# Three narrow attention stages of an eight-layer kernel: score lanes regrouped into five slots, and extra matmuls at the head of a stage

## The reference, cut to what matters

```
q = norm(x) @ Wq + bq ; k = ctx @ Wk + bk ; v = ctx @ Wv + bv      # 16 heads of 8
p = softmax(q k^T * scale [+ mask])                                # 512 x 154 for a head
x = x + tanh(gate) * (p v @ Wo + bo)
```

## Time and profile before

| | us |
|---|---|
| median of the three runs | 2459.78 |
| the profiled execution | 2450.34 |
| its span, first to last instruction | 2448.6 |
| TensorE busy | 2070.1 (85%) |
| VectorE busy | 1224.5 (50%) |
| ScalarE busy | 702.1 (29%) |
| mean granted TensorE clock | 0.857 of full |

### The profile page before, as it was taken

The page is one execution under the profiler, slowest core; times in us unless marked ns, Lnnn a source line. Parts: engine busy times, 40 slices in busy tenths (PEclk is TensorE's granted clock), DMA queues, the critical chain, the costliest instruction groups (busy, mean ns, idle before and its releaser), DMA issues. The chain is left out here.

```text
span 2448.6 us, 33104 instructions
## 1 busy us (share of the span) xinstructions
PE 2070.1 (85%) x12226; PEld 1166.4 (48%) x12226; DVE 1224.5 (50%) x2940; ACT 702.1 (29%) x1245; POOL 93.2 (4%) x178
## 2 busy tenths in 40 slices
PE   4689799988898987987799788888888796997997
PEld 3343477763534435554544344444444554543554
DVE  5553222226655655554443364736364575342776
ACT  2332233332233331222132313142422222323221
POOL 0000000000000000000000101010101001000000
PEclk7777899999898998997597688898989876787999
DMA  1320000020000000000000000000000000000000
GB/s 35 111 77 6 1 0 0 0 48 17 0 0 0 0 0 0 0 0 6 14 9 1 0 1 2 1 2 1 1 1 1 1 0 14 14 1 1 1 0 17
DMA packets 36509, 23.68 MB, mean 10 GB/s; under 512 B 14275, under 2 KB 31896, under 8 KB 36405
## 3 DMA queue, kind: packets, MB, share of 16 engines
q1 hardware_dynamic: 34965, 21.93, 3.6%
q10 hardware_dynamic: 1440, 0.29, 0.1%
HBM read 16.04 MB, written 1.05 MB: 7 GB/s over the span
## 5 line engine op out<-in xcount | busy, mean ns | idle before, releaser
L1741 ACT ACTIVATE L2a_qwork<-psum 128x512 f32<-128x512 f32 (+3 forms) x256 | 94.5, 438 | 226.8 <-PE psum L1671 225.4
L452 DVE RECIPROCAL L1x_rsum<-psum 128x512 f32<-128x512 f32 x32 | 107.4, 3356 | 84.1 <-PE psum L343 84.1
L1842 DVE RECIPROCAL L2a_rsum<-psum 128x512 f32<-128x512 f32 x16 | 53.7, 3357 | 153.4 <-PE psum L1686 153.4
L1340 ACT ACTIVATE L0f_hid<-psum,L0f_b 128x512 f32<-128x512 f32 x128 | 87.9, 687 | 142.3 <-PE psum L1292 140.1
L395 ACT ACTIVATE L1x_pT<-psum 77x512 f32<-77x512 f32 x128 | 68.8, 587 | 193.8 <-PE psum L329 193.7
L1305 PEld LDWEIGHTS psum<-expert_arena,L0f_hid 128*128 128x128 f32 x1024 | 118.4, 192 | 12.0 <-issue 11.5
L1292 PE MATMUL psum<-L0f_xnT,expert_arena 128*128 128x512 f32 x256 | 122.7, 625 | 0.0
L1667 PE MATMUL psum<-L2a_qT,L2a_kT 64*128 64x128 f32 (+3 forms) x512 | 108.2, 506 | 15.2 <-ACT L2a_qwork L1741 10.7
L1305 PE MATMUL psum<-expert_arena,L0f_hid 128*128 128x128 f32 x1024 | 119.3, 275 | 0.0
L1455 DVE SCALAR_TENSOR_TENSOR L0f_acc<-psum,L0f_comb,L0f_acc 128x128 f32<-128x128 f32 x128 | 36.0, 344 | 159.4 <-PE psum L1305 159.4
L1824 DVE TENSOR_REDUCE L2a_negmax<-psum 128x2 f32<-128x256 f32 (+3 forms) x128 | 100.8, 821 | 24.3 <-PE psum L1639 24.3
(11 more groups left out here) (553 smaller groups left out, 3948.0 us busy)
## 6 DMA issues: line engine op xcount, KB each, us to landing
expert_arena<-in_L_ffn_w SPq DMA_DIRECT2D x16, 256.0 KB
L1f_gu<-in_L_ffn_gate_up_w SPq DMA_DIRECT2D x8, 256.0 KB, 4.1
resid<-in_x SPq DMA_DIRECT2D x4, 256.0 KB, 6.1
L0x_q<-L0x_qc SPq DMA_DIRECT2D x16, 64.0 KB
L1f_dn<-in_L_ffn_down_w SPq DMA_DIRECT2D x8, 128.0 KB, 4.2
expert_arena<-in_L_ffn_w_gate_up SPq DMA_DIRECT2D x2, 512.0 KB, 5.4
L2x_q<-L2x_qc SPq DMA_DIRECT2D x16, 64.0 KB
L3x_q<-L3x_qc SPq DMA_DIRECT2D x16, 64.0 KB
```

Source lines behind the costliest of these rows:

```text
L452: v.step(nc.vector.reciprocal(rsum[:, g % 2, :], psum[:, 2 * (g % 2) + 1, :]))
L1340: nc.scalar.activation(hid[0:rows, n % RING, :], psum[0:rows, n % 4, :], ACT.Relu, bias=bias).then_inc(s["hid"], 1)
L1741: nc.scalar.activation(pT[:, c % 2, j, PLACE[k]:PLACE[k] + WIDTH[k]], psum[:, 4 + n % 4, k * P:SEQ], ACT.Exp, scale=scale).then_inc(s["pt" ...
```

## The change

Within the three narrow stages:

- The transposed scores go in five slots for each batch. Slots 0 to 3 take the four row groups of one plane c side by side, into four banks (2 to 5). Slot 4 takes the last 26 keys as 16 tiles of 32 rows by 32 columns, straight from k4, so that `kbd` and GpSimd's work on it go. `values` is split into `products` and `sums`, which are called one slot later and apart from each other.
- Banks 2 and 3 are thereby taken from the score units. Every unit now writes banks 0 and 1, and unit n waits for the reduce of unit n - 1. The projections share bank 0 (`FRONT`) and bank 1 (`OUT`) with the units.
- The maxima go in halves of a batch (planes 0 and 1, then 2 and 3), with a `max_rows`, a copy and a DMA for each.
- `turned(f)` moves from the end of a batch to the head of the next one, behind `products` and `sums` of the last slot. VectorE's `squares` and `rotated` move with it, behind `normalised(b-1)`.
- `output(b-1)` comes after the first slot but one. bo and bv no longer cost one-row matmuls: GpSimd adds gate * (bv @ wo + bo) to the residual beforehand. wo is loaded with its rows regrouped.
- `warm(6)` at the head of the stage and `warm(4)` ahead of the first score units issue ten matmuls of 128x128 by 512 whose result is not used.

```diff
+    FRONT, SUMS, OUT = 0, 7, 1
...
+            def warm(n):
+
+                for _ in range(n):
+                    nc.tensor.matmul(psum[:, SUMS, :], core.ident[:], core.ctxT[:, 0:SEQ], start=True, stop=True)
+
+            warm(6)
...
-                    if n >= 2:
-                        pe.wait_ge(s["mx"], UNITS * f + n - 1)
+                    if n:
+                        pe.wait_ge(s["mx"], n)
...
-                            last = nc.tensor.matmul(psum[:, j, (t % 2) * CTX:(t % 2 + 1) * CTX], q4[rows, f % QB, c, t * P:(t + 1) * P],
+                            last = nc.tensor.matmul(psum[:, j % 2, (t % 2) * CTX:(t % 2 + 1) * CTX], q4[rows, f % QB, c, t * P:(t + 1) * P],
...
+                if c < NG:
+                    for j in range(NG):
+                        rows = slice(32 * j, 32 * j + 32)
+                        if n:
+                            pe.wait_ge(s["pt"], NG * (n - 1) + j + 1)
+                        nc.tensor.matmul(psum[:, 2 + j, :], k4[rows, b, c, 0:MAIN], q4[rows, b % QB, c, :], start=True, stop=True).then_inc(s["s2"], 1)
+                    return
+                for x in range(NG):
+                    for j in range(NG):
+                        rows = slice(32 * j, 32 * j + 32)
+                        if x == 0:
+                            pe.wait_ge(s["pt"], NG * (n - 1) + j + 1)
+                        last = nc.tensor.matmul(psum[32 * x:32 * x + 32, 2 + j, :], k4[rows, b, x, MAIN:KP], q4[rows, b % QB, x, :], start=True, stop=True)
```

More of the change, by code:

```diff
@@ L849, in _ @@
                 queries(0)
+                if masked:
+                    for x in range(2):
+                        last = nc.tensor.transpose(psum[0:64, 2, x * KH:(x + 1) * KH], pen_w[:, x].rearrange("p b h -> p (b h)"), core.ident[0:KH, 0:KH])
+                    last.then_inc(s["pen_ps"], 1)
+                if not rope:
+                    nc.tensor.matmul(psum[:, 6, 0:D], bvb[:], w["wo"][:], start=True, stop=True).then_inc(s["bias_ps"], 1)
                 turned(0)
+                contexts(1)
@@ new lines, in _ @@
+                    n = 16 * f
+                    scoresT(b, 0)
+                    if b:
+                        max_rows(2 * b + 1)
+                        products(b - 1, NG)
+                        sums(b - 1, NG)
+                    else:
+                        scores(8, 16)
+                    if f < B:
+                        turned(f)
+                    if b == 0:
+                        max_rows(1)
+                    scoresT(b, 1)
+                    if b:
+                        output(b - 1)
@@ new lines, in _ @@
+                    if f < B:
+                        scores(n, n + 2)
+                    products(b, 0)
+                    if f < B:
+                        scores(n + 2, n + 3)
+                    sums(b, 0)
+                    if f < B:
+                        scores(n + 3, n + 4)
+                    scoresT(b, 2)
+                    if f < B:
+                        scores(n + 4, n + 5)
+                    products(b, 1)
+                    if f < B:
+                        scores(n + 5, n + 6)
@@ new lines, in _ @@
+                    sums(b, 1)
+                    if f < B:
+                        scores(n + 6, n + 8)
+                    scoresT(b, 3)
+                    products(b, 2)
+                    if f < B:
+                        max_rows(2 * f)
+                    sums(b, 2)
+                    if f < B:
+                        scores(n + 8, n + 12)
+                    if g < B:
+                        contexts(g)
+                        rowsT(g)
+                    scoresT(b, 4)
+                    if g < B:
+                        queries(g)
@@ L880, in _ @@
+                    products(b, 3)
+                    if f < B:
+                        scores(n + 12, n + 13)
+                    sums(b, 3)
+                    if f < B:
+                        scores(n + 13, n + 16)
+                products(B - 1, NG)
+                sums(B - 1, NG)
                 output(B - 1)
```

485 lines of the change are left out of this document (232 added, 253 removed).

## The result

| | before | after |
|---|---|---|
| median of the runs | 2457.02 us (2449.64 to 2462.27) | 2537.5 us (2535.61 to 2541.84) |
| profiled execution, its span | 2450.3, 2448.6 | 2536.5, 2534.8 |
| granted clock, mean | 0.857 | 0.848 |
| L0x, L2x, L3x | 251.4, 234.0, 218.5 | 296.6, 245.6, 241.9 |

The ratio is 1.0332, with a 95% interval of 1.03 to 1.0365: slower. The three narrow stages are 45.2 + 11.6 + 23.4 = 80.2 us longer, of the span's 86.2.

A forecast was written before the change was run, and what follows sets the result against it. TensorE was taken to set the pace, by its work and its clock. The profiled 2450.3, less 1 at full clock, plus 70 for the clock, gave 2519, on the median's scale 2530; range 2475 to 2590, whole range 2400 to 2610.

The forecast's parts named there:

- Turns: Score units in two banks: TensorE and VectorE alternate, 1.7 us a unit at full clock, 2.3 at clock 0.5.
- The head of L0x: Batches 1 and 2 of L0x: 26.3 us ahead of the units, with squares and rotated now behind normalised(b-1).
- Batch 3: Last batch of each narrow stage, dense without score units: 21.6 us, from 38.8, 40.4 and 35.5.
- Slot 4: Last transposed scores of a batch as 32x32 tiles: 1.9 us instead of 3.6.
- my two bounds: For slot 4: one block, 0.93 us, or no overlap between column groups, 3.7 us.
- The clock: Batches 0 to 2 of the three stages lose clock: +70 us, 81 less some 10 for the fronts; bounds 0 and +170.
- The sums at full clock: Change in time per narrow stage without clock loss: L2x -8, L3x -12, L0x +19, together -1 us.
- Half of the time at 0.5: Batches 0 to 2 spend about half the time at clock 0.5: 9 us for each of nine batches, 81.
- The ten extra matmuls: Warm passes in each stage's front: cost nothing beside other work, no gain in the batches.
- Rival 1: Whole kernel: clock stays full, most new waits being 1.15 us; sum -1, time 2459, chance 0.14.
- Rivals 2 and 3: Rival 2: turn waits under 0.5 us, 2399, chance 0.14. Rival 3: clock 0.5 throughout batches 0 to 2, 2630, chance 0.12.

The follow-up runs named there:

- experiment 1: Kernel before, with its score units confined to two banks, each waiting for the maxima of the unit before: 2682.7 us, ratio 1.0926.
- experiment 4: Changed kernel with the first eight units of a stage in four banks, each waiting for the unit before the last: 2508.2 us, ratio 1.0217.
- experiment 3: Changed kernel with VectorE's squares and rotation of the next batch ahead of the reciprocal of the batch before: 2526.2 us, ratio 1.0275.
- experiment 2: Changed kernel with products against a tile of zeros (fillings) ahead of each unit that waits bare: two fillings 2561.7 us, one filling 2524.4 us.
- experiment 6: Changed kernel with rotation ahead of the reciprocal, units 0 to 7 in four banks, one filling per bare wait from unit 9 on: 2476.5 us, ratio 1.0075.
- experiment 9: Kernel before, last batch's transposed scores in four banks, plus unused full-height passes in front waits: twelve 2400.2 us, last three alone 2402.9; twelve with 32x32 fifth slot 2416.0.

## Why the prediction was right, and where its steps were not

The forecast of 2530 us (range 2475 to 2590 for its own case) met 2537.5. By its steps:

- **Turns.** 1.7 and 2.3 us were forecast and measured to the digit. That turns cost this much is shown by experiment 1, where they alone cost 227 us, and experiment 4 gives 29 us back, 25 of them in the fronts.
- **The head of L0x.** Forecast 26.3 us in batches 1 and 2, measured 26.8 and 27.1. The order of rotation and reciprocal in it is worth 11 us (experiment 3).
- **Batch 3.** Forecast 21.6 us at full clock, measured 26.1, 24.4 and 25.9 at 0.86 to 0.93, and 22.7 in L2x where it had full clock (experiment 2, two fillings). So the work was right within some 1 us, and that the clock would be below full here as well was left out: most of the 12 us that the three are above the forecast. Slot 4 was forecast at 1.9 and is 1.08: of my two bounds the lower one held. The Trainium skill's TensorEngine Tiling (Array Packing), Key Properties, has tiles operate independently, and the trace agrees for these sixteen: 1.08 us, against 0.97 for a block of four abreast.
- **The clock.** The sums at full clock were -8, -12 and +19 us for L2x, L3x and L0x; measured were +11.6, +23.4 and +45.2. The difference is 81 us, where I had put 70 on the clock. It lies where the forecast put it: the nine batches 0 to 2 are 78 us above their sums at full clock (81 were forecast), the last batches 12 above, and the fronts and tails 9 below (10 were forecast). An estimate from experiment 2 gives 59 of the 78 to the clock. Batch 0 of L2x, forecast at 57 us with full clock, took 65.7 at 0.67, and 55.8 at 0.94 in experiment 6, cut in the same way. The other 19 us weren't taken apart; full clock throughout was never reached in any run. Half of the time at 0.5 was a guess without a rule behind it. It came out (0.66 to 0.80), and in that there is luck: two executions of one stream differed by more than 10 us a batch (experiment 6). Outside the three stages the profiled execution is 6 us longer, in code that isn't changed.
- **The ten extra matmuls.** Forecast at nothing, with "no gain in the batches". Without them the kernel takes 13 us more, 5 of them in the fronts and 3 in the batches; 4 lie in unchanged code. I had priced what they cost in their waits and not that the projections behind them, and in L0x the first units, run at full clock.
- **Rival 1,** the clock stays full because the waits are short, is wrong as a mechanism. In experiment 2, with one filling, almost no wait was left in the front of L2x and the clock stayed at 0.50. The Trainium skill, TensorE: Matmul & The Clock Gate, Why this matters for your kernels, asks for a TensorE that is busy without long gaps. The trace doesn't agree that this is always enough: busy 24.7 of 25 us at 0.50, with score units of two row groups in between.
- **Rivals 2 and 3.** Turns never overlapped better than 1.70, and the clock was at neither bound: 0.66 to 0.80 in the nine batches.

## What to carry to other kernels

Before giving up buffers to make room for a denser step, price the turn that producer and consumer then take: here batches 0 to 2 lost 153 us (a part of it the eight units that moved there from each front) where the dense last batches won 38, and as much was to be had alone, in the one batch where banks were free. Where TensorE waits anyway, full-height work in the wait that is last before a dense stretch is worth a try: three passes there made batch 0 of L2x a quarter shorter, and four that idle time followed did nothing. Then add up the whole stage, since later batches took most of that back. And read the granted clock beside every window before crediting an edit with a difference: an untouched batch moved by 9 us.

## What was not expected of the hardware

- At equal work both clock levels hold: the same stream of units that use two row groups and of full-height fillings, with next to no gap, ran for 25 us at 0.50 (experiment 2) and for 12 us at full clock in another run (experiment 6), whose own batch 0 of L3x had 0.50 for its first 43 us. What decides is open.
- Units alone, two at a time, are at 2.30 us a pair in the fronts of L2x of every kernel of which I read the timeline. Right behind passes they are faster for a while: one pair at 1.69 in L2x in experiment 9, three at 1.70 in L0x in experiment 4.
- Turn-taking costs more in clock than in waits: by the estimate above 12 to 14 us against 8, of the 23 in batch 1 of L2x (experiment 1).
